# Two graph layers on one core: the stretch between the layers in units of ten columns, own features added by block

## The reference, cut to what matters

```python
# x (6250, 96); 200000 edges src -> dst, sorted by dst; edge_attr (200000, 96)
h = relu(layernorm(x))
msg = relu(h[src] + edge_attr @ W_edge.T + b_edge)
u = relu(((1 + eps) * h + segment_sum(msg, dst)) @ W1.T + b1)
x = x + u @ W2.T + b2                       # layer 0

h = relu(layernorm(x))
m = h[src] + 1e-7
a = exp(m) / segment_sum(exp(m), dst)[dst]  # softmax over a node's edges
x = x + (h + segment_sum(a * m, dst)) @ W + b   # layer 1
```

## Time and profile before

| | |
|---|---|
| median of 3 runs | 2506.68 us (2506.21 to 2509.19) |
| the profiled execution | 2505.36 us, span 2503.6 us |
| granted TensorE clock, mean | 0.874 of full speed |
| TensorE matmul busy | 1874.7 us, 75% |
| VectorE busy | 1846.6 us, 74% |
| ScalarE busy | 772.3 us, 31% |
| GpSimd busy | 1503.2 us, 60% |

### The profile page before, as it was taken

One profiled execution on the slowest core, in us unless ns is written; L12 is line 12 of the kernel. 1 busy time (PEld: TensorE's weight loads), 2 busy tenths in 40 slices (PEclk: granted clock), 3 DMA queues, 4 the chain that ended last, 5 costly groups with the idle time before them and its releaser, 6 DMA issues.

```text
span 2503.6 us, 54920 instructions
## 1 busy us (share of the span) xinstructions
PE 1874.7 (75%) x11673; PEld 1561.1 (62%) x11674; DVE 1846.6 (74%) x4248; ACT 772.3 (31%) x1316; POOL 1503.2 (60%) x1556
## 2 busy tenths in 40 slices
PE   3777777776676767577676776776667677999999
PEld 2466666665565656466565665655555566888887
DVE  8999998878787888778787878887877883222232
ACT  5001121222233333344444444445445552000000
POOL 4777777777777777777777777777777600000000
PEclk9899898888888888888888888788888878999999
DMA  5234344444444444454544445454455424656553
GB/s 160 50 83 105 94 116 104 115 114 110 124 114 117 120 119 125 117 143 118 138 124 134 130 131 145 136 136 138 135 134 139 121 79 170 216 195 213 203 205 134
DMA packets 150484, 332.03 MB, mean 133 GB/s; under 512 B 58051, under 2 KB 108253, under 8 KB 134446
## 3 DMA queue, kind: packets, MB, share of 16 engines
q1 hardware_dynamic: 29758, 166.84, 22.3%
q0 software_dynamic: 49248, 75.74, 13.7%
q10 hardware_dynamic: 71258, 87.51, 10.2%
HBM read 242.47 MB, written 87.48 MB: 132 GB/s over the span
## 4 chain that ended last, share of the span: by engine, by line
POOL 55%; PE 19%; issue 19%; DMA 3%; DVE 3%; ACT 1%; POOLq 0%; DVEq 0%; ACTq 0%; SPq 0%
POOL rows_buf L522 55%; PE ps L775 16%; DMA rows_buf<-table,index 2%; PE ps L608 1%; DVE ps L1216 1%; ACT features_buf L838 0%; PE ps L700 0%; PE ps L597 0%; PE ps L789 0%; DVE zone L1330 0%; DVE zone L1253 0%; PE ps L754 0%; DMA xs<-x 0%; PE ps L783 0%; POOLq L527 0%
## 5 line engine op out<-in xcount | busy, mean ns | idle before, releaser
L522 POOL DMA_INDIRECT rows_buf<-table,index x1539 | 1488.0, 967 | 495.6 <-issue 491.9
L700 PE MATMUL ps<-zone,planes 128*128 128x400 f16 x2352 | 614.9, 377 | 537.1 <-DVE zone L1253 425.8
L1253 DVE TENSOR_SCALAR zone<-iota_c,planes 128x400 f16<-128x400 int16 x2352 | 673.0, 339 | 59.9 <-issue 49.1
L896 ACT ACTIVATE features_buf<-ps 128x800 f16<-128x800 f32 x392 | 327.8, 836 | 1214.6 <-PE ps L700 1209.3
L700 PEld LDWEIGHTS ps<-zone,planes 128*128 128x128 f16 x2352 | 251.1, 107 | 715.3 <-issue 657.8
L597 PEld LDWEIGHTS ps<-wet,zone 128*128 128x128 f32 x3136 | 543.7, 248 | 43.8 <-issue 32.4
L597 PE MATMUL ps<-wet,zone 128*128 128x96 f32 x3136 | 530.6, 327 | 8.5 <-DMA zone<-edge_t 8.5
L584 PE MATMUL ps<-onehot,features_buf 128*96 128x128 f32 x3120 | 421.2, 280 | 0.0
L584 PEld LDWEIGHTS ps<-onehot,features_buf 128*96 128x96 f32 x3120 | 387.4, 171 | 11.2 <-issue 1.1
L1216 DVE TENSOR_TENSOR ps<-ps,rows_buf 128x768 f32<-128x768 f32 x171 | 164.5, 962 | 240.1 <-DMA rows_buf<-table,index 211.0
L1018 DVE TENSOR_TENSOR planes<-ps,planes 128x1536 f16<-128x1536 f32 x196 | 341.2, 1741 | 0.0
(11 more groups left out here) (162 smaller groups left out, 595.7 us busy)
## 6 DMA issues: line engine op xcount, KB each, us to landing
counts<-features_buf ACTq DMA_DIRECT2D x392, 200.0 KB
zone<-edge_t SPq DMA_DIRECT2D x98, 768.0 KB
rows_buf<-counts SPq DMA_DIRECT2D x32, 1600.0 KB, 6.3
single<-table SPq DMA_DIRECT2D x3072, 0.4 KB
planes<-counts SPq DMA_DIRECT2D x17, 1600.0 KB, 6.2
rows_buf<-table,index POOLq DMA_INDIRECT x1539
final<-residual ACTq DMA_DIRECT2D x48, 48.0 KB, 3.5
out<-final ACTq DMA_DIRECT2D x48, 48.0 KB, 3.9
```

Of the source, the lines that this page charges most:

```text
L522: nc.gpsimd.indirect_dma_start(out=into[:, t, :], out_offset=None, in_=table, in_offset=bass.IndirectOffsetOnAxis(ap=at[:, t:t + 1], axis= ...
L700: nc.tensor.matmul(count_ps[:, bass.ds(banks[k], WC)], row_hot[:, u % 2, g * GS + k, :], pair_hot[:, g * GS + k, :], start=False, stop=Fal ...
L896: nc.scalar.activation(count_out[:, k], bank, ACT.Copy, accum_out=row_sum[:, bass.ds(p, 1)]).then_inc(moved, 1)
L1253: last = nc.vector.tensor_scalar(pair_hot[:, k, :], iota_c[:, :], step_pair[:, bass.ds(i * (IS * SC) + (u * SC + k), 1)], None, ALU.is_equal)
```

## The change

`uT` is written column by column, so that `node_layer` reads each column's nodes side by side. b2 is no longer a 97th row: it is broadcast into `bias2` and added to `xs` by five VectorE instructions in the last turn of layer 0's loop; GpSimd fills no ones on this branch. The flag is made before the node layer's results and loaded early by each engine. The transposes of `hs`, and the copies to `h1t`, are gone from the fast branch; `hs` is stored to a DRAM table `hidden` by units, and each block's 128 own rows are loaded to `own` and added to the message in `softmax`. The first three buffers of counts are loaded as soon as they are free: block 0 with the flag, blocks 1 and 2 after the last `add_node`, ahead of the residual's store. The table of layer 1 is made in five units of ten columns, with the f16 of e taken by GpSimd and the rests made by VectorE in one instruction each (scaled and written as f16); exp carries the factor 2048 in its bias. ScalarE makes the last two units of features between these steps. Blocks 0 and 1 are summed together, unit by unit, as the table's units come.

```diff
                 sp.wait_ge(node_out, NG)
+                for b in (1, 2):
+                    block_load(b, b)
                 for part in (slice(0, EVEN), slice(EVEN, NP)):
                     sp.dma_start(residual.rearrange("(p j) d -> p j d", j=NJ)[part], xs[part, :, :]
                                  ).then_inc(residual_out, 16)
-                sp.wait_ge(parts_ready, 1)
-                for b in (1, 2):
-                    block_load(b, b)
+                for u in range(NU):
+                    sp.wait_ge(features, NU + u + 1)
+                    for part in (slice(0, EVEN), slice(EVEN, NP)):
+                        sp.dma_start(hidden.rearrange("(p j) d -> p j d", j=NJ)[part, units[u], :],
+                                     hs[part, units[u], :]).then_inc(own_out, 16)
+                sp.wait_ge(own_out, 2 * NU * 16)
+                sp.wait_ge(step_done, SC + NSTEP)
+                for b in range(2):
+                    sp.dma_start(own[:, b, :], hidden[b * P:(b + 1) * P, :]).then_inc(own_in[b], 16)
...
-            pool.wait_ge(add_done, RS + NC)
-            nc.gpsimd.memset(rows_buf[D:P, 0:N], 1.0).then_inc(ones_ready, 1)
-            pool.wait_ge(step_done, SC + NSTEP)
-            nc.gpsimd.memset(zone[D:P, NS * CE:NB * P], 1.0).then_inc(ones_ready, 1)
...
+            with pool.Else():
+                for u in range(NU):
+                    pool.wait_ge(fexp_ready, u + 1)
+                    nc.gpsimd.tensor_scalar(table16[0:NP, units[u], 2 * D:3 * D], exps[:, u % NE], 1.0 / LO_SCALE, None,
+                                            ALU.mult).then_inc(exp_high, 1)
...
-                                                by_column(inputs)[:, g * JG + k, :], weight[:, :],
+                                                inputs[:, g * JG + k, :], weight[:, :],
...
-            node_layer(hidden_out, N // UC, uT, w2s, 0)
-            pe.wait_ge(node_out, NG)
-            transposes(1)
+            node_layer(hidden_out, N // UC, uT.rearrange("f (j p) -> f j p", j=NJ), w2s, 0)
...
-                pe.wait_ge(ones_ready, 2)
-                block_sums(0, 0, 1)
-                block_sums(1, 1, 1)
+                for b in range(2):
+                    pe.wait_ge(block_in[b], 16)
+                for u in range(NU):
+                    pe.wait_ge(exp_high, u + 1)
+                    pe.wait_ge(exp_low, u + 1)
+                    pe.wait_ge(weighted_high, u + 1)
+                    pe.wait_ge(parts_ready, u + 1)
+                    for b in range(2):
+                        for j in range(u * UN, (u + 1) * UN):
+                            last = nc.tensor.matmul(
+                                ps[:, b, 0:4 * D], blocks[b][0:NP].rearrange("p (d j) -> p j d", j=NJ)[:, j, :],
+                                table16[0:NP, j, :], start=(j == 0), stop=(j == NJ - 1))
+                        if u == NU - 1:
+                            last.then_inc(block_ps, 1)
                 turn(0, 0)
...
+            flag = fast_of(act)
+            deviation_of(1, 0)
+            for u in range(1, NU):
+                deviation_of(1, u)
+                if u < NU - 1:
+                    feature(1, u - 1)
...
+                def product_high(u):
+                    act.wait_ge(weighted_ready, u + 1)
+                    nc.scalar.activation(table16[0:NP, units[u], 0:D], products[:, u % NW2], ACT.Copy,
+                                         scale=1.0 / LO_SCALE).then_inc(weighted_high, 1)
+
+                act.wait_ge(step_done, SC + NSTEP)
+                exp_of(0)
+                exp_of(1)
+                exp_of(2)
+                product_high(0)
+                product_high(1)
+                feature(1, NU - 2)
+                exp_of(3)
+                product_high(2)
+                feature(1, NU - 1)
+                exp_of(4)
+                product_high(3)
+                product_high(4)
...
-                def residual_load(b, u, rows_at, n=P):
+                def residual_load(b, u, rows_at, n=P, first=False):
+                    if not first:
+                        act.dma_start(own[0:n, u % BU, :], hidden[rows_at, :]).then_inc(own_in[u % BU], 16)
...
                 act.wait_ge(residual_out, 32)
+                act.wait_ge(own_out, 2 * NU * 16)
...
+                if u0 == NS:
+                    dve.wait_ge(w_in, 16 * 9)
+                    dve.wait_ge(features, NU)
+                    for u in range(NU):
+                        nc.vector.tensor_tensor(
+                            xs[:, units[u], :], xs[:, units[u], :],
+                            bias2[:, :].rearrange("p (a d) -> p a d", a=1).to_broadcast([NP, UN, D]), ALU.add
+                        ).then_inc(bias_added, 1)
...
-                nc.vector.tensor_scalar(uT[0:D, k * UC:(k + 1) * UC], ps[0:D, k % HB, 0:UC], b1c[:, 0:1], 0.0,
-                                        ALU.add, ALU.max).then_inc(hidden_out, 1)
+                nc.vector.tensor_scalar(uT.rearrange("f (j p) -> f p j", j=NJ)[:, k * UP:(k + 1) * UP, :],
+                                        ps[0:D, k % HB, 0:UC].rearrange("f (p j) -> f p j", j=NJ), b1c[:, 0:1],
+                                        0.0, ALU.add, ALU.max).then_inc(hidden_out, 1)
+            dve.wait_ge(bias_added, NU)
...
+            flag = fast_of(dve)
...
+                    nc.vector.scalar_tensor_tensor(products[:, u % NW2], hs[:, units[u], :], P_SCALE, exps[:, u % NE],
+                                                   ALU.mult, ALU.mult).then_inc(weighted_ready, 1)
...
+                    nc.vector.scalar_tensor_tensor(table16[0:NP, units[u], 3 * D:4 * D],
+                                                   table16[0:NP, units[u], 2 * D:3 * D], -LO_SCALE, exps[:, u % NE],
+                                                   ALU.mult, ALU.add).then_inc(exp_low, 1)
...
+                    nc.vector.scalar_tensor_tensor(table16[0:NP, units[u], D:2 * D], table16[0:NP, units[u], 0:D],
+                                                   -LO_SCALE, products[:, u % NW2],
+                                                   ALU.mult, ALU.add).then_inc(parts_ready, 1)
+
+                weigh(0)
+                weigh(1)
+                exp_rest(0)
+                exp_rest(1)
+                product_rest(0)
+                weigh(2)
+                product_rest(1)
+                exp_rest(2)
+                weigh(3)
+                product_rest(2)
+                exp_rest(3)
+                weigh(4)
+                product_rest(3)
+                exp_rest(4)
+                product_rest(4)
...
-                                                   ).then_inc(soft_done, 1)
+                                                   ).then_inc(soft_step[5], 1)
+                    dve.wait_ge(soft_step[5], b + 1)
+                    dve.wait_ge(own_in[u % BU], (i + (u // BU + 1)) * 16)
+                    nc.vector.tensor_tensor(soft[:, slot, 3, 0:D], soft[:, slot, 3, 0:D], own[:, u % BU, :], ALU.add
+                                            ).then_inc(soft_done, 1)
...
-                    nc.vector.tensor_tensor(node_t[0:D, slot, :], h1t[0:D, bass.ds(b * P, P)], ps[0:D, 2 + slot, 0:P],
-                                            ALU.add).then_inc(soft_added, 1)
+                    nc.vector.tensor_copy(node_t[0:D, slot, :], ps[0:D, 2 + slot, 0:P]).then_inc(soft_added, 1)
```

127 lines of the change are left out of this document (69 added, 58 removed).

## The result

The changed kernel takes 2483.2 us (median of 4 runs, 2481.6 to 2484.0), beside 2506.4 us for the kernel before on the same chip (2505.7 to 2509.2): a ratio of 0.9897, 95% interval 0.9885 to 0.9910, so 23.2 us faster. The prediction said 2484.0 and a range of 2476 to 2493.

The account below looks back on a forecast made before the run. GpSimd's gathers bound layer 0's loop and TensorE's matmuls the blocks; the change edits the 97 us between. Terms -3.1 + 2.4 - 2.7 - 19.4 + 0.25 = -22.6 us gave 2482.8 profiled, median 2484, range 2476 to 2493.

Parts of the forecast that it names:

- The loop's additions: Layer 0's loop: five additions of b2 cost VectorE 5.9 us, hidden by its waits, so taken as 0.
- The cover named: Layer 0's loop: after the additions VectorE waits 11.0 us for gathered rows alone, and gathers run eight chunks ahead.
- The loop's end: Before the hidden layer: without GpSimd's fill VectorE's one-hots are not held and TensorE starts earlier, -3.1 us.
- The hidden layer: Stepped writes of uT cost 0.20 us more in each of 25 instructions, partly eaten by waits: +2.4 us.
- The node layer: Packed weight loads instead of stepped ones, the step and not the clock being the limit: -2.7 us.
- its other bound: Node layer: if the clock falls, TensorE paces it at about 0.27 us and 100 loads take 5 us longer.
- The table and the first blocks: Last deviation to block 2: 52.1 us become 32.7, VectorE's limit with GpSimd's time added in full, -19.4 us.
- a sign of being wrong: Table: GpSimd instructions over 2 us were listed among what would show the forecast wrong; 1.7 us was taken.
- the first two rivals: Table: GpSimd works beside VectorE without exclusion, 2479.6 us (chance 0.15); GpSimd at 3.4 us a unit, 2492.6 (0.13).
- the third rival: First blocks: the clock stays at 1.2 GHz, 100 matmuls take 32.6 us, 2496.9 in all; chance 0.07.
- the slower one: Blocks: own rows arrive late and every block waits; 1 us a block gives 2531; chance 0.04.
- Tail: End of the kernel: one more addition in the last softmax, +0.25 us.

Follow-up runs that it names:

- experiment 7: The changed kernel run again unedited, on the chip of the later runs: 2488.5 us, before 2510.8 on that chip, ratio 0.9900.
- Experiment 9: Against the changed kernel, the five additions of b2 made six times over: 2502.9 us, ratio 0.9964 to the kernel before, 14.5 us above the changed kernel.
- experiment 10: Against the changed kernel, b2 back in the product, its row of ones written by ScalarE: 2481.0 us (first run); with e's rounding shared by ScalarE and GpSimd too: 2477.5 us.
- experiment 4: Against the changed kernel, GpSimd's fill of ones put back beside the additions: 3652.6 us, before 3665.5, ratio 0.9951.
- experiment 2: Against the changed kernel, uT written in node order again and read with a step by the node layer: 3709.7 us, ratio 0.9922 to the kernel before.
- experiment 6: Against the changed kernel, VectorE's first table instruction waits until GpSimd has rounded three units alone: 3647.1 us, ratio 0.9945 to the kernel before.
- experiment 8: Against the changed kernel, b2 added by GpSimd after the loop, e's rounding shared by ScalarE (units 0, 4) and GpSimd (1 to 3): 2488.7 us, ratio 0.9906.
- the ScalarE variant: Against the changed kernel, ScalarE instead of GpSimd makes the five f16 parts of e: 3720.8 us, ratio 0.9942 to the kernel before.

## Why the prediction was right, term by term

**The loop's additions** were the term that was missed: costed at 0, they took 2.4 us of the 2.6 by which the loop ends later. The cover named, VectorE's waits for rows, is real for VectorE; what the step left out is the engine beside it. In the changed kernel:

```profile
1896.01 1.51 POOL L542 DMA_INDIRECT rows_buf<-table,index  x1 [0.30 <-issue]
1897.82 1.83 POOL L542 DMA_INDIRECT rows_buf<-table,index  x1 [0.30 <-issue]
1899.96 1.84 POOL L542 DMA_INDIRECT rows_buf<-table,index  x1 [0.30 <-issue]
1902.10 0.95 POOL L542 DMA_INDIRECT rows_buf<-table,index  x1 [0.30 <-issue]
```

These three gathers stand beside the five additions (1895.55, 5.42 us) and lose 0.57 + 0.89 + 0.90 = 2.4 us, and GpSimd is what binds the loop. In experiment 7's trace of the same kernel it is two gathers, of 1.90 and 1.83 us, that lose 1.9. (A single gather of 1.0 to 1.5 us turns up now and then in every trace, that of the kernel before too; but of the gathers after the first 110 us, in the seven traces where the gathers bind, those over 1.5 us stand beside additions alone.) Experiment 9 raises the loss with the number of additions, experiment 10 takes it away. What in an addition holds a gather was not taken apart; additions with one input in PSUM, as in every chunk of the loop, stand beside gathers of 0.94 us.

**The loop's end**: right, -3.8 against -3.1, shown by experiment 4. What was late next was VectorE's queue, as expected (its L1370 releases the hidden layer): the one-hots are done at 2004.2, and two additions of 0.28 us and the queue's signal come after them.

**The hidden layer**: mis-sized, -0.7 against +2.4. The price of a single instruction was right: with the step it lasts 0.66 us (median 657 ns), without it 0.47 (474 in experiment 2), 0.19 more. But neighbours overlap: back to back they stand 0.53 apart, not 0.43, so the step costs 0.1 us an instruction, and it eats waits first; experiment 2 prices it at 0.7 us. TensorE's first eight matmuls took 1.90 us, not 3.10, at a clock of 1.00, and that gave 1.2 back. TensorE had paused 1.2 us before them, not 4.05; with the fill put back it paused 5.3 us and took 3.62. The pause alone does not decide it, though: after 1.8 to 1.9 us three runs took 1.90 us and five took 2.6 to 3.2.

**The node layer**: the number was close, 1.8 against 2.7 us, but not by the mechanism given. The step in the read limited it before, and at a clock of 1.00 the packed loads do take 0.19 us. But the clock fell to 0.54 in 2022 to 2024 and to 0.50 after it, which the prediction held as its other bound, at +5 us. A packed load at the low clock takes 0.33 us, as long as the stepped load did at either clock (0.31), but loads follow each other 0.21 us apart, not the 0.27 of that bound, and this is just VectorE's pace (4.2 us a unit of twenty loads), so the loss stayed small. Where the clock held, in experiment 10's first run, the same stretch takes 22.2 us, 4.0 less than before. Experiment 2 gives 2.4 for the packed read.

**The table and the first blocks**: -21.0 against -19.4, though GpSimd's price was wrong. It needs 2.6 us alone and up to 3.6 when it starts behind a VectorE instruction, not 1.7, and over 2 us is a sign of being wrong that the prediction names itself; but the engines hold each other up only in part (experiment 6), where the sum let all of GpSimd's time add. The two errors cancel, which is luck: 11.95 us to unit 0 against 2.3 + 9.6 = 11.9 predicted. What released unit 0 was no sum of five VectorE instructions and two of GpSimd, but a chain: two roundings from 2047.44 to 2053.60, the rest of e of unit 1 to 2055.56, the rest of w of unit 0 to 2056.63. Experiments 8 and 10 take the roundings out of it, and unit 0 comes after 7.8 and 7.7 us. And the limit that set the end was TensorE's (31.6 us in the prediction), not VectorE's (32.7): its matmuls run from 2056.78 to 2074.63 without a pause, and block 2 follows 1.26 us later. With full exclusion, GpSimd's 5 x 2.6 = 13 us in place of 8.5, the same sum would have been 37 us, and it was 31.06. So the truth was a mixture of the first two rivals, each wrong alone. Neither the third rival (from 2059.84 on ten matmuls take 1.79 us, the full clock's pace) nor the slower one was met: the first own rows, whose loads were issued at 2068.98 and took 1.9 us to land, are used at 2075.27. That is 4.4 us to spare, not the 10 predicted. The Trainium skill (SBUF — State Buffer, Who interferes with whom) has the two engines exclude each other when a VectorE instruction with two SBUF inputs meets a GpSimd one that reads SBUF. The trace agrees one way only: a rounding that starts 0.05 us behind a VectorE instruction of 1.16 us takes 3.58 us in place of 2.6, but a VectorE instruction that starts behind a rounding's start takes 1.93 us in place of 1.15 and ends before it. The near total stop is seen for another kind of instruction, the 16-bit one-hots, beside the fill (6.93 us against 2.18) and beside GpSimd's additions (6.18 us for three).

**Tail**: +0.86 against +0.25. From the last VectorE instruction to the end, which is the last store, it is 3.5 us against 2.9; the last softmax chain takes 3.99 us against 3.96.

## What to carry to other kernels

A wait of the engine that does the added work is not the whole cover: look at which other engine its instructions slow down, and above all at whether that is the engine that binds. When a table is made for one user, let the user start with the first unit: that gave 12.0 to 12.7 of the 21.0 us here, as long as no unit came late; in the ScalarE variant one did, and the clock fell with it. Where two prices are unknown, a sum can be right through two errors; only the parts, each measured alone, tell which.

## What the runs showed of the hardware

- VectorE additions of 125x960 float values, both inputs in SBUF, stretch GpSimd's indirect gathers from 0.94 to 1.84 us, once to 1.90.
- GpSimd rounds 960 values a partition from f32 to f16 in 2.59 us alone (2.7 ns a value) and adds 960 pairs in 2.2 us; while it adds, f16 one-hot instructions of VectorE make almost no progress (6.18 us for three), and VectorE's instructions that read PSUM keep their pace (0.49 us apart).
- A rounding by GpSimd waits for a VectorE instruction with two SBUF inputs that has started before it (3.58 us in place of 2.6 behind one of 1.16); the other way round VectorE loses 0.8 us, not the rounding's 2.6.
- ScalarE writes single rows of 1250 values, one after the other, in 1.16 us each, and nobody waited for them.
- A VectorE instruction that writes 250 values with a step of 500 bytes lasts 0.66 us in place of 0.47, but back to back only 0.1 us of that is seen.
- Reading weights with a step costs TensorE 0.31 us a load at either clock; a packed load of nearly the same size takes 0.19 us at the full clock and 0.33 at the low one. The clock held at 1.00 for most of the node layer was worth 2.3 us (21.5 against 23.8). Why it held in two runs (experiment 8 and the first of experiment 10) and fell in the others, three of which have the first's hidden layer of 14.3 us, stays open.
